# Modulation gates clamped as columns instead of rows, and the written order of the first stages of an adaLN transformer block

## The reference, cut to what matters

```python
mod = (_silu(c) @ wmod).reshape(2, 6, 1, 512)
sa, ca, ga, sb, cb, gb = mod[:, 0], ..., mod[:, 5]
ga = (2 * (ga >= 0) - 1) * jnp.maximum(jnp.abs(ga), 0.25)
gb = (2 * (gb >= 0) - 1) * jnp.maximum(jnp.abs(gb), 0.25)
h = _layernorm(x) * (1 + ca) + sa
x = x + ga * attn(h)     # conv of 3 taps 512 -> 3*128, q k v of 16 heads x 64, causal
                         # softmax in blocks of 128, output product, @ proj_w + proj_b
h = _layernorm(x) * (1 + cb) + sb
x = x + gb * ffn(h)      # h @ base_w.T + base_b + 0.5 * (top-2 of 16 experts, rank 64)
```

## Time and profile before

| | |
|---|---|
| median of 3 runs | 470.56 us (470.47 to 470.79) |
| profiled execution: time | 470.41 us |
| profiled execution: span of the instructions | 468.4 us |
| PE busy | 420.9 us (90%) |
| DVE busy | 356.3 us (76%) |
| ACT busy | 302.0 us (64%) |
| POOL busy | 268.8 us (57%) |
| mean granted TensorE clock | 0.984 |

### The profile page before, as it was taken

One profiled execution on the slowest core, in us unless ns is written; L12 is line 12 of the kernel. 1 busy time (PEld: TensorE's weight loads), 2 busy tenths in 40 slices (PEclk: granted clock), 3 DMA queues, 4 the chain that ended last, 5 costly groups with the idle time before them and its releaser, 6 DMA issues.

```text
span 468.4 us, 11145 instructions
## 1 busy us (share of the span) xinstructions
PE 420.9 (90%) x4170; PEld 270.2 (58%) x4170; DVE 356.3 (76%) x675; ACT 302.0 (64%) x974; POOL 268.8 (57%) x309
## 2 busy tenths in 40 slices
PE   3589949989989999999999999999897979888976
PEld 0265527666677656776667766666474744453432
DVE  4769989897978889878878786768867896646531
ACT  2445567987888798688568867666876866522210
POOL 4220726311775677756448776667528779976271
PEclk9799979999999999999999999999999999999999
DMA  8999763352474669536738836556842264672532
GB/s 318 235 397 388 207 206 46 59 123 47 80 147 113 158 133 202 143 84 115 181 72 157 163 49 145 111 139 117 156 115 46 47 136 90 153 142 45 136 80 77
DMA packets 144901, 65.09 MB, mean 139 GB/s; under 512 B 134704, under 2 KB 134960, under 8 KB 144464
## 3 DMA queue, kind: packets, MB, share of 16 engines
q1 hardware_dynamic: 144704, 64.37, 57.7%
q10 hardware_dynamic: 144, 0.02, 0.1%
HBM read 26.63 MB, written 4.19 MB: 66 GB/s over the span
## 4 chain that ended last, share of the span: by engine, by line
PE 51%; DVE 16%; POOL 10%; DMA 9%; ACT 6%; issue 5%; SPq 2%; ACTq 0%; POOLq 0%; DVEq 0%
PE F L1024 15%; PE C L1133 12%; PE C L1024 10%; PE W L1024 3%; PE S L1179 3%; PE W L1196 3%; ACT prob L705 3%; DMA xa<-in_x_dram 3%; POOL prob L584 2%; DVE p L915 2%; DMA gT<-g 2%; PE S L1024 2%; DMA xb<-in_x_dram 2%; DVE nm L909 2%; DVE qk L895 2%
## 5 line engine op out<-in xcount | busy, mean ns | idle before, releaser
L1133 PE MATMUL C<-hT,cw 128*128 128x256 f16 x864 | 108.4, 277 | 13.0 <-DVE cv L886 6.9
L584 POOL TENSOR_TENSOR prob<-prob,rinv 128x1024 f32<-128x1024 f32 x32 | 62.4, 1948 | 73.7 <-DVE rinv L920 73.7
L1133 PEld LDWEIGHTS C<-hT,cw 128*128 128x128 f16 x864 | 83.0, 99 | 32.1 <-issue 7.4
L705 ACT ACTIVATE prob<-S,nms 128x128 f32<-128x128 f32 x256 | 89.9, 377 | 7.1 <-DVE p L915 6.0
L1024 PE MATMUL F<-btw,gT 128*128 128x512 f16 x336 | 74.8, 379 | 2.2 <-DMA gT<-g 2.1
L676 ACT ACTIVATE qk<-C,bqk 128x256 f16<-128x256 f32 x128 | 52.6, 479 | 14.2 <-PE C L1024 13.4
L895 DVE SCALAR_TENSOR_TENSOR qk<-C,bqk,qk 128x256 f16<-128x256 f32 x128 | 54.3, 474 | 4.6 <-ACT qk L676 4.6
L1024 PEld LDWEIGHTS F<-btw,gT 128*128 128x128 f16 x336 | 32.5, 98 | 40.7 <-DMA gT<-g 2.9
L705 ACT ACTIVATION_READ_ACCUMULATOR prob<-S,nms 128x1 f32 x256 | 55.5, 217 | 0.0
L1024 PE MATMUL C<-cv,pw 128*128 128x256 f16 x384 | 50.4, 273 | 2.4 <-DVE cv L886 1.9
L915 DVE SCALAR_TENSOR_TENSOR p<-prob,p 128x1024 f16<-128x1024 f32 x32 | 48.3, 1509 | 4.6 <-ACT p L714 4.3
(11 more groups left out here) (187 smaller groups left out, 722.2 us busy)
## 6 DMA issues: line engine op xcount, KB each, us to landing
xa<-in_x_dram SPq DMA_DIRECT2D x10, 512.0 KB, 4.3
xb<-in_x_dram SPq DMA_DIRECT2D x6, 512.0 KB, 5.0
wmb<-in_wmod_dram SPq DMA_DIRECT2D x1, 3072.0 KB, 19.1
out_dram<-xb SPq DMA_DIRECT2D x12, 256.0 KB, 2.4
cw_raw<-in_cw_dram SPq DMA_DIRECT2D x3, 768.0 KB, 5.3
raw<-in_cw_dram SPq DMA_DIRECT2D x3, 768.0 KB, 5.2
wma<-in_wmod_dram SPq DMA_DIRECT2D x4, 512.0 KB, 6.9
bt_raw<-in_btw_dram SPq DMA_DIRECT2D x2, 1024.0 KB, 9.7
```

What stands on the lines that cost most here:

```text
L584: nc.gpsimd.tensor_tensor(prob[:], prob[:], rinv[:, i % 2].unsqueeze(2).broadcast_to([P, 8, P]), ALU.mult).then_inc(p_normal, 1)
L705: ins = nc.scalar.activation(prob[:, h], S[i % len(S)][h // 4][:, (h % 4) * P:(h % 4 + 1) * P], ACT.Exp, bias=nms[:, i % 2, h:h + 1], scal ...
L1133: ins = nc.tensor.matmul(bank_c[:, 0:CH], cw[:, i, a, c, tap, :], hT[:, j % 2, b, c, OWN - 1 + tap:OWN - 1 + tap + CH], start=step == 0, s ...
```

## The change

Four things change together. The gates are clamped as columns: `row:0:2` and `row:0:3` only copy their rows; `cols:0:1` and a new `cols:0:2` transpose the gate rows too, and DVE clamps 128 x 8 numbers. `pick:0:0` to `pick:0:3` spread a gate by an identity product: four float32 matmuls, whose weights are a gate column repeated 128 times. The first gate's row is made once, not twice. The second chunk's `hs` becomes two stages, one for each block, so that SP issues the load of `cw_raw` 2 between the two transposes. The second half of `pj` becomes its own stage `pk`. And SCHEDULE is another one over its whole length.

```diff
-        na:0:0 sil:0:0 halo:0:0 nb:0:0 na:1:0 hs:0:0 row:0:0 nb:1:0 hs:1:0 cols:0:0 sp:0:0 c:0:6 sp:0:1 sp:0:2 c:0:9
-        halo:1:0 c:0:18 vb:0:0 na:2:0 vb:0:1 sp:0:3 c:0:9 sp:0:4 c:0:24 nb:2:0 c:0:3 qk:0:0 c:0:3 qk:0:1 sp:0:6
-        row:0:2 qk:0:4 qk:0:5 c:0:24 pick:0:0 pick:0:1 sp:0:5 c:0:12 qk:0:2 s:0:0 hs:2:0 m:0:0 qk:0:3 na:3:0 v:0:2
-        v:0:0 e:0:0 nz:0:0 row:0:3 c:1:3 halo:2:0 pj:0:0 c:1:6 s:0:1 m:0:1 ph:0:0 qk:0:6 c:1:3 qk:0:7 c:1:21 nb:3:0
-        bias:0:0 c:1:3 e:0:1 c:1:3 nz:0:1 c:1:3 s:0:2 xr:0:0 pj:0:1 c:1:3 m:0:2 c:1:6 ph:0:1 na:4:0 c:1:3 sp:0:8
+        na:0:0 sil:0:0 nb:0:0 na:1:0 hs:0:0 row:0:0 nb:1:0 cols:0:0 hs:1:0 sp:0:0 halo:0:0 halo:1:0 hs:1:1 c:0:33
+        sp:0:1 sp:0:2 vb:0:0 na:2:0 vb:0:1 sp:0:3 c:0:9 sp:0:4 c:0:6 sp:0:5 c:0:24 qk:0:2 qk:0:1 row:0:2 nb:2:0
+        qk:0:4 c:0:9 cols:0:2 qk:0:5 c:0:6 qk:0:0 c:0:3 pick:0:0 pick:0:1 c:0:3 pj:0:0 c:0:3 na:3:0 c:0:9 s:0:0
+        m:0:0 sp:0:6 c:0:3 row:0:3 hs:2:0 pk:0:0 e:0:0 nz:0:0 v:0:2 qk:0:3 qk:0:6 s:0:1 m:0:1 ph:0:0 qk:0:7 v:0:1
+        e:0:1 pj:0:1 halo:2:0 cols:0:1 c:1:15 nz:0:1 c:1:15 bias:0:0 c:1:3 pk:0:1 c:1:3 v:0:0 v:0:3 s:0:2 c:1:6
...
-        gh:3:0 qk:6:2 qk:6:3 fb:3:1 pr:4:1 s:6:0 m:6:0 pr:4:0 ph:5:3 c:7:3 G:3:1 c:7:3 l2a:4:0 c:7:3 sp:0:14 ra:0:4
...
+        gh:3:0 s:5:2 fb:3:1 m:5:2 ph:5:1 qk:6:5 sp:0:14 wo:4:0 G:3:1 e:5:2 xr:4:0 fb:3:0 nz:5:2 pr:4:0 ra:0:4 v:5:2
...
+        sel = ident[:].rearrange("p (q i) -> p q i", q=4)[:, :, 0:NB]
...
+        h_blocks = lambda j, n: (n,) if j == 1 else (0, 1)
...
-                    for b in range(2):
+                    for b in h_blocks(j, n):
...
-                    if j < 2:
-                        sp.dma_start(cw_raw[:, j + 1], cw_in[:, j + 1]).then_inc(ld[f"cw{j + 1}"], 16)
+                    if j + n < 2:
+                        sp.dma_start(cw_raw[:, j + n + 1], cw_in[:, j + n + 1]).then_inc(ld[f"cw{j + n + 1}"], 16)
...
-            def clamp(rows, at, to):
-                g, a, b = rows[at:to, :], tmprow[at:to, 0], tmprow[at:to, 1]
+            def clamp(g, columns):
+
+                a, b = tmpcol[:, 0], tmpcol[:, 1]
+                link(nc.vector.tensor_copy(g, columns))
...
+                    if n > 0:
+                        ins = clamp(gate[:, 2 - n], at[:, rows - 1, :, 0:NB])
...
+                elif s == "pk":
                     dve.wait_ge(pj_hi, n + 1)
...
-                        for i, m in enumerate([(0, 1), (), (2, 2), (0, 1, 2)][n]):
+                        for i, m in enumerate([(0, 1), (), (2,), (0, 1, 2)][n]):
...
+                    if n < 4:
+
+                        for k in range(DC):
+                            ins = nc.tensor.matmul(m_bank(stage)[:, k * P:(k + 1) * P],
+                                                   gate[:, n // 2, k, b:b + 1].broadcast_to([P, P]), ident[:],
+                                                   start=True, stop=True)
```

## The result

The changed kernel takes 475.78 us (median of 6 runs, 475.0 to 477.39) against 470.51 (6 runs, 468.72 to 471.95) of the kernel before on the same chip: ratio 1.0107, 95% interval 1.0076 to 1.0137. It is about 5 us slower, where 467.0 was forecast. The profiled executions, on which the readings of traces rest, are 6.9 us apart, 1.6 more than the medians: 477.33 against 470.41.

The account below looks back on a forecast made before the run. PE, busy 90% of 468.4 us, was taken as the bound, its holes the only thing to win. Gains 2.7 + 1.7 + 1.7 less 2.7 made 3.4 us: 470.41 - 3.4 = 467.0 us, range 462.0 to 471.8.

Parts of the forecast that it names:

- DVE's clamp: Both gate clamps on DVE, 2.30 + 5.74 us, become five operations on columns at 1.0 us each, 2.0 for both.
- Picks: PE's new gate picks cost 1.5 us more for the first two and 0.6 for the two later ones.
- Until 34 us: Start of the kernel: nothing gained, the first cv not ready before 33.88 us; bounds 0 and 0.6 gained.
- The second gap: PE's wait for chunk 2's transposes behind 3 MB of loads: 60.8 to 63.9 us, 3.1 long; net 2.7 us gained.
- I take 63.0: Chunk 2's first transpose lands at 63.0 us, between 57.5 if it overtakes the loads and 64.5 with whole latency behind them.
- the second rival: The start is spent: PE's early idleness drops the clock, -1.7 us, and one later stretch gives nothing back; 470.4 us, chance 0.15.
- 3.3 us gained: PE's gain by the end of s:0:2, at 68.5 instead of 70.6 us: 2.1 ahead plus 1.2 more work done.
- After 70 us: Rest of the list: 1.7 us back at 100 to 140, 1.7 at 320 to 400, 2.7 lost at sp:0:14, tail 0.
- My own sign of being wrong: Wrong if transposes land at once, first cv precedes 33, or PE's waits from 100 to 400 us differ far from 12.
- 100 to 140 and 320 to 400: PE's standing there falls by a third of 5.0 us and a quarter of 6.8 us, 1.7 us each.
- `sp:0:14`: Near 300 us ACT waits 5.3 us for fb:3:0 before this split, and PE then stands 2.7 us at pr:4:0.
- The rival on this wait: Slower: nothing on PE covers ACT's lateness at sp:0:14, so PE loses 8.4 us, clock included; 472.7 us, chance 0.20.

Follow-up runs that it names:

- experiment 1: Changed kernel with hs:2:0 back ahead of row:0:3, so chunk 2's transposes are issued before the 3 MB of loads: 482.18 us, ratio 1.0197.
- experiment 2: Changed kernel with xr:2:0 moved behind nz:3:2: 472.66 us, ratio 1.0023 to the kernel before.
- experiment 3: Changed kernel with sp:0:14 moved behind pr:4:0: 480.79 us, ratio 1.0172 to the kernel before.
- experiment 6: Changed kernel with hs:2:0 ahead of row:0:3 and each bt_raw half load issued behind a transpose of p: 471.14 us, ratio 0.9998.
- experiment 9: Kernel of experiment 6 with xr:2:0 also moved behind nz:3:2: 468.65 us, ratio 0.9933 to the kernel before.
- experiment 10: Kernel of experiment 9 with fb:3:0 also moved ahead of sp:0:14: 467.13 us, ratio 0.9919 to the kernel before.
- experiment 11: Changed kernel, list untouched, with only the two bt_raw loads each issued behind a transpose of p: 467.98 us, ratio 0.9913.
- experiment 13: Kernel of experiment 11 with xr:2:0 behind nz:3:2 and fb:3:0 ahead of sp:0:14: 467.0 us, ratio 0.9898 to the kernel before.
- experiment 14: Control: the kernel before with only the two bt_raw loads each issued behind a transpose of p: 471.34 us, ratio 0.9995.
- experiment 7: Changed code with the new list up to chunk 2 and the old list behind it: 481.7 us, ratio 1.0168 to the kernel before.
- experiment 5: The kernel before with hs:2:0 moved behind row:0:3, so the 3 MB of loads go first: 477.33 us, ratio 1.0124.
- experiment 8: Changed code with the old list first, to e:2:1, and the new list behind it: 477.49 us, ratio 1.0126 to the kernel before.

## Why the prediction was wrong

Its steps, one by one:

- **DVE's clamp: right.** Five operations of 0.16 or 0.17 us, 0.2 apart, 1.0 us in all, in both clamps. DVE's rows of the first, in after:

```profile
42.78 0.16 DVE L779 COPY gate<-F 128x8 f32<-128x8 f32 x1
...
43.58 0.17 DVE L783 SCALAR_TENSOR_TENSOR gate<-tmpcol 128x8 f32<-128x8 f32 x1
```

- **Picks: too dear.** The first two took 1.95 us together, +0.8 instead of +1.5. The two later ones take 1.05 and 1.16 where the old took 1.12, so the further 0.6 was nothing. By the Trainium skill, page "TensorE: Matmul & The Clock Gate", section "LDWEIGHTS (loading the stationary operand)", a weight load costs by its columns and not by its rows; the trace agrees as far as a pick goes: four times the loads, each with four times the rows, cost no more.
- **Until 34 us: off by 1.4 us.** The first `cv` product starts at 35.28, not 33.88. The x of chunk 2 landed at 31.33 instead of 29.93. But experiments 1, 2, 3, 6, 9, 10, 11 and 13 have the same code and list until then, and their product starts at anything from 33.77 (9) to 35.25 (6); with the list of before it is 33.88 in before and 34.69 in experiment 14. So the 1.4 us are no more than what differs from run to run, and a cause in the change is not shown.
- **The second gap: the step that failed first, by its size.** The mechanism was right and so were the times around it: `row:0:3` at 49.74 (49.0 forecast), PE out of work at 60.9 (60.8). "I take 63.0" for the landing of the transposes was the mis-sized term: the first landed at 65.7, 2.7 us later than taken and later even than the 64.5 at which I had put its whole latency behind the loads, and the wait ended at 66.2, not 63.9, after 5.25 us and not 3.1. Of the 2.7 us, 1.8 are in the loads. They were issued at 53.43, 0.6 later than forecast, and were through at about 63.0 and not 61.2: from 54 to 62 us 32 of the DMA's 374 packets are under 512 bytes, and from 63 to 66 us 2044 of 2051 are, which are those of the transposes. The sum had a slip too: it read the 9.3 us of before from 54.0, which is 0.8 after the issue, and then counted its 8.4 from the issue itself. The other 0.9 is the latency, 2.7 us behind the loads where I took 1.8. And 5.25 us let the clock fall, which I had put into the second rival at 1.7 us: PE ran at 1.2 GHz from 66.2 to 71.1, 2.5 us more for the same work. In place of "3.3 us gained" at 70 us, `s:0:2` ended at 72.8 against 70.6. Experiment 11 takes 2 MB away from ahead of the transposes and gets 7.8 us back, the 4.5 us of the wait and the 2.5 of the clock in the main.
- **After 70 us: the step that failed altogether.** From "between these PE's own work sets the time, and what PE gains early is kept" I reasoned over the stretch from 140 to 320 us as if it held for the new list too. It is a property of the old list's order, not of the work: the new one has 15.4 us of waits there, 13.8 with the early loss mended, 13.1 with the old start, and the old list's middle has 0.2 even behind the new start (experiment 7). My own sign of being wrong names it: PE's waits between 100 and 400 us add up to 17.8 us, not to about the 12 of before. One place in it is shown, `xr:2:0` with SP's reload ahead of a transpose and POOL's 8.37 us, and experiment 2 gave some 3 to 4 us back for it, though experiment 13 not on top of the spread loads. I had looked at the distance from `fl` to `xr` for chunks 4 and 5 and not for 2. The other waits there are not traced to a cause.
- **100 to 140 and 320 to 400: the other way.** I gave PE back 1.7 of 5.0 and 1.7 of 6.8. It stood 1.65 us in the first (3.3 forecast) and 0.7 in the second (5.1), 9.4 less in all, where I took 3.4. The stretches hold other work than before, so this is not all gain.
- **`sp:0:14`: right in size, and with a clock fall on top.** ACT stood 4.43 us for `fb:3:0` (5.3 forecast) and PE 2.72 at `pr:4:0` (2.7): two high halves, one low half behind them and two halves of `att`, as forecast. PE's timeline of after:

```profile
316.46 1.12 PE L1025 MATMUL C<-pjw,att 128*128 128x512 f16 x3 [2.72 <-DVE att L931]
```

  The clock was at 0.50 from 316.9 to 320.3, which the sum did not hold; 1.7 us. The rival on this wait priced it at 8.4 and was not what made the kernel slower. Experiment 3 moved the split instead of mending the wait, and experiment 10 took the wait down to 1.1 us without a gain that is clear of noise.

So the kernel came out slower by two losses, of which the forecast had one at 3.1 us of its 5.25 and without its clock, and the other not at all. With the first removed by moving two loads, the change gives 467.98 us (experiment 11), close to the 467.0 of the forecast; but that is luck, a sum of other parts: more was won at the start and after 320 us, and lost in the middle.

## What to carry to other kernels

Here a DMA transpose behind 3 MB of plain loads in the same queue waited for them, its issue too, and held all that stood behind it in the queue. When a word of an order is moved, list what its DMA part is moved past, and keep large loads from standing ahead of a transpose that the bounding engine needs (here PE waited 0.76 us with 1 MB ahead and 0.55 with none, and 2 MB more cost 8 us of time). That an engine never waits in a stretch says nothing about another order of the same work: a new order's waits have to be read from its own dependences, first of all at the instructions that wait for a reload with other work queued behind them. A wait of PE is not worth its length: removing one of 5 us, or one that set a unit back by 7, handed it on to the next in the queue, and spreading the loads gave back 8. The clock fall behind a wait can cost more than the wait itself adds, as in experiment 5.

## What the runs showed of the hardware

- **The issue of a transpose blocks behind loads.** Two transposes of a chunk: 2.61 us of issue with 1 MB ahead, 8.77 with 3 MB; 7.31 in experiment 5. By the Trainium skill, page "DMA: Bandwidth & Descriptors", section "Queues, rings and completion order", each DMA engine consumes the descriptors of a ring in order, while a later transfer may still complete first. The trace agrees with the first half: the packets of the transposes moved from 62 us on, when the loads were nearly through, and no run here shows the second. SP itself stood in the issue of the second transpose of after for 4.93 us, and nothing behind it was issued.
- **The low clock follows some short waits of PE and not others of the same length.** In after, the fall at the wait of 5.25 us cost 2.5 us of busy time and the one behind 2.72 us cost 1.7. At `pv:3:1` waits of 3.15 and 3.34 us (experiments 3 and 6) were followed by a fall, and waits of 3.02, 3.27 and 3.39 us at the same place (11, 8 and after) were not. A wait of 2.36 us near 454 us was followed by one in experiment 14 and not in the kernel before. Each such fall cost 1.5 to 1.7 us, and it is part of what separates one profiled run from the next.
- **One form on DVE has two durations.** A clamp operation over 32x512 took 2.17 us where one over 64x512 took 0.68. The slow one began while POOL was at its product of 53.83 to 55.73 us; POOL had no work during the fast one. Whether that is the cause was not tried.
